# Depthwise taps and layer 3's context in tiles of 32 rows and columns, with new orders and PSUM banks

## The reference

```python
x = x + L0(gn(x))   # attention over rows of C, softmax of 256x256 scores per image
x = x + L1(gn(x))   # batch norm, sign, grouped 3x3 convolution, batch norm, PReLU
x = x + L2(gn(x))   # below
x = x + L3(gn(x))   # linear attention, 8 heads of 16 channels
# L2
h = depthwise_conv3x3(x, dw_w) + dw_b
h = prune(relu(bn(h)), 4.0)         # a channel whose maximum is under the limit becomes 0
h = conv1x1(h, pw_w) + pw_b
h = prune(relu(bn(h)), 0.001)
# L3, per image and head
k = softmax(k, axis=-1)
context = einsum('bhdn,bhen->bhde', k, v)
out = einsum('oc,bcn->bon', w_out, einsum('bhde,bhdn->bhen', context, q)) + b_out
```

## Time and profile before

| | us |
|---|---|
| median of 3 runs | 74.31 (74.23 to 74.63) |
| profiled execution | 74.13 |
| its span | 72.4 |
| TensorE busy | 59.6 (82%) |
| VectorE busy | 47.3 (65%) |
| ScalarE busy | 33.0 (46%) |
| GpSimd busy | 23.9 (33%) |

### The profile page before, as it was taken

How to read it: one execution, slowest core, us unless ns; L and a number is a source line. 1 busy time by engine, 2 the same in 40 slices (tenths; PEclk the granted TensorE clock), 3 DMA queues, 4 the chain that set the end, 5 groups by cost and what they waited for, 6 DMA issues and landing times.

```text
span 72.4 us, 1449 instructions
## 1 busy us (share of the span) xinstructions
PE 59.6 (82%) x472; PEld 46.2 (64%) x472; DVE 47.3 (65%) x182; ACT 33.0 (46%) x98; POOL 23.9 (33%) x67
## 2 busy tenths in 40 slices
PE   3995999799999999399988997899366989968530
PEld 2763787688989878188955663656145869945210
DVE  3959859565688979844579845919869764343430
ACT  5103973958947000570377422402809958642200
POOL 6608899889933335100110043000051340000000
PEclk9999999999999999999999999999999999999995
DMA  0695000000000000000000000000000000002222
GB/s 0 182 407 155 0 0 0 0 0 5 0 0 9 5 0 0 0 0 0 0 0 9 5 0 0 0 9 0 0 0 0 0 5 0 0 9 72 72 72 72
DMA packets 2136, 1.97 MB, mean 27 GB/s; under 512 B 592, under 2 KB 1872, under 8 KB 2128
## 3 DMA queue, kind: packets, MB, share of 16 engines
q1 hardware_dynamic: 2128, 1.87, 7.8%
HBM read 1.35 MB, written 0.52 MB: 26 GB/s over the span
## 4 chain that ended last, share of the span: by engine, by line
PE 53%; DVE 20%; POOL 9%; issue 5%; DMA 5%; ACT 2%; SPq 1%; POOLq 0%; ACTq 0%; DVEq 0%
PE bank L1486 11%; PE bank L1431 6%; PE bank L1418 5%; DMA x<-in_x 5%; POOL gn_rstd L352 4%; DVE t L759 4%; PE bank L1394 4%; PE bank L1560 3%; PE bank L1620 3%; PE bank L1600 3%; PE bank L1405 2%; DVE x L1177 2%; PE bank L1445 2%; PE bank L1579 2%; PE bank L1570 2%
## 5 line engine op out<-in xcount | busy, mean ns | idle before, releaser
L352 POOL TENSOR_TENSOR gn_rstd<-gn_var_eps,minus_half 128x1 f32<-128x1 f32 (+2 forms) x11 | 6.9, 631 | 25.4 <-DVE gn_var_eps L1122 8.5
L1317 PE MATMUL bank<-warm 128*128 128x256 bf16 x36 | 6.7, 349 | 1.2 <-POOL warm L337 1.2
L1317 PEld LDWEIGHTS bank<-warm 128*128 128x128 bf16 x36 | 4.4, 126 | 2.4 <-POOL warm L337 1.2
L1431 PE MATMUL bank<-signs,conv_blocks 128*128 128x256 bf16 x36 | 4.3, 276 | 1.2 <-ACT signs L539 1.2
L539 ACT ACTIVATE signs<-res,bn_shift,bn_scale 128x256 bf16<-128x256 f32 x4 | 2.2, 595 | 6.4 <-DVE bn_shift L932 6.4
L1486 PE MATMUL bank<-t,dw_diag 64*64 64x256 f32 x72 | 4.3, 381 | 0.7 <-DVE t L1046 0.7
L1486 PE MATMUL bank<-x,dw_diag 64*64 64x256 f32 x72 | 4.6, 383 | 0.3 <-DVE x L991 0.3
L1431 PEld LDWEIGHTS bank<-signs,conv_blocks 128*128 128x128 bf16 x36 | 3.4, 97 | 2.2 <-issue 1.6
L1445 PE MATMUL bank<-valid,dw_diag 128*128 128x256 f32 x18 | 4.5, 388 | 0.0
L1394 PE MATMUL bank<-k,q 128*128 128x256 f32 x16 | 4.3, 389 | 0.2 <-DVE k L841 0.2
L1418 PE MATMUL bank<-vt,probT 128*128 128x128 f32 x32 | 4.4, 280 | 0.0
(11 more groups left out here) (196 smaller groups left out, 156.7 us busy)
## 6 DMA issues: line engine op xcount, KB each, us to landing
out<-x SPq DMA_DIRECT2D x4, 128.0 KB, 1.7
late_params<-in_late SPq DMA_DIRECT2D x1, 404.5 KB, 4.5
x<-in_x SPq DMA_DIRECT2D x1, 384.0 KB, 3.4
...
l_params<-in_late SPq DMA_DIRECT2D x3, 4.5 KB, 2.6
```

Of the source, the lines that this page charges most:

```text
L352: return nc.gpsimd.tensor_tensor(out_ap, in_ap, minus_half[:, 0:n], ALU.pow)
L1317: nc.tensor.matmul(bank[:, 0:N], warm[:, 0:C], warm[:, :], start=True, stop=True)
L1431: ins = nc.tensor.matmul(conv_ps[b], conv_w[:, tap, :], signs[:, b, dy:dy + H, dx:dx + W], start=(tap == 0), stop=(tap == TAPS - 1))
```

## The change

- Both pairs' taps run on the raw images in tiles of 32 rows and 32 columns. A row tile r of pair 0 writes the partitions of columns `2i + r % 2`, one of pair 1 those of `2i + 1 - r % 2`; rows 0 and 1 share a bank, and so do rows 2 and 3. The taps of pair 1 stand between those of pair 0. `norm2` and `t2` are gone, and both pairs get `less_mean` and `dw_scale`.
- The channels of pair 1 come out swapped by 32, so `pw2` and the constants of layer 2 get swapped copies by eight more DMAs, and the group sums a swapped matrix `group_swap`.
- `dw_diag` has 32 columns, and one GpSimd operation writes it instead of nine of ScalarE. It needs `ident_tile`, which VectorE makes first of all its statistics. Variances and roots of layer 2, the sums of layer 3 and the reciprocals move to GpSimd.
- The mask's taps run in four diagonal 32x32 tiles.
- In layer 3 all images are handled one by one. Context and its projection run in four tiles of 32 rows; the context has two banks, and so has the output.
- The orders of the tail change on every engine. ScalarE runs `negative_part(2)` ahead of the first square sum, and `relu1(1, 0)` ahead of `square_sum3(0)`.

In the diff a line "..." stands for what is left out.

```diff
     dw_ps = [[banks[i][:, 0:N] for i in pair] for pair in ((3, 4), (0, 1))]
-    pw_ps = [banks[6][:, 0:N], banks[2][:, 0:N]]
+    pw_ps = [banks[i][:, 0:N] for i in (6, 2, 3, 4)]
...
-    k3_ps = [banks[(3, 4)[b % 2]][:, 0:N] for b in range(B)]
+    k3_ps = [banks[(6, 2)[b % 2]][:, 0:N] for b in range(B)]
...
-    pj_ps = banks[2][:, 0:C]
-    y_ps = banks[6][:, 0:N]
+    pj_ps = banks[4][:, 0:C]
+    y_ps = [banks[(6, 2)[b % 2]][:, 0:N] for b in range(B)]
...
-    cx_ps = banks[7][:, 0:C]
+    cx_ps = [banks[(7, 3)[b % 2]][:, 0:TILE] for b in range(B)]
...
+        pw_swap = late[:, LC["pwT"]].rearrange("(r s p) o -> s p r o", r=2, s=2)
+        l2_swap = late[:, first:first + 9].rearrange("(r s p) f -> s p r f", r=2, s=2)
+        for quarter in range(TILES):
+            to = slice(quarter * TILE, (quarter + 1) * TILE)
+            side = 1 - quarter % 2
+            sp.dma_start(pw2[to, 2:4, :], pw_swap[side]).then_inc(halves_in, 16)
+            sp.dma_start(l2p[to, 3:5, :], l2_swap[side]).then_inc(halves_in, 16)
...
-            pool.wait_ge(halves_in, 16 * 5)
+            pool.wait_ge(halves_in, 16 * 13)
...
-                                    ALU.mult, ALU.add)
-            nc.gpsimd.memset(t2[:, :, :, :], 0.0).then_inc(l2_consts, 1)
+                                    ALU.mult, ALU.add).then_inc(l2_consts, 1)
...
+        def group_swaps():
+            there = group_swap[:, :].rearrange("p (h s o) -> p s h o", h=2, s=2)
+            here = group_avg[:, :].rearrange("p (h s o) -> p s h o", h=2, s=2)
+            for side in range(2):
+                ins = nc.gpsimd.tensor_scalar(there[:, side], here[:, 1 - side], 1.0 / N, 0.0,
+                                              ALU.mult, ALU.add)
+            ins.then_inc(group_swap_ready, 1)
+        def dw_diagonals():
+            pool.wait_ge(late_in, 16)
+            pool.wait_ge(ident_tile_ready, 1)
+            nc.gpsimd.tensor_tensor(
+                dw_diag[:, :, :], ident_tile[:, :].unsqueeze(1).to_broadcast([C, TAPS, TILE]),
+                lp[:, LC["dw"]].unsqueeze(2).to_broadcast([C, TAPS, TILE]),
+                ALU.mult).then_inc(dw_diag_ready, 1)
...
+        def gn2_mean_diag(p):
+            pool.wait_ge(group_read[2], p + 1)
+            nc.gpsimd.tensor_tensor(
+                mean_diag[:, p, :, :], ident_tile[:, :].unsqueeze(1).to_broadcast([C, 2, TILE]),
+                gs2[:, p, 4:6].unsqueeze(2).to_broadcast([C, 2, TILE]),
+                ALU.mult).then_inc(mean_diag_ready, 1)
+        def gn2_scale(p):
+            pool.wait_ge(group_read[2], p + 1)
+            step(nc.gpsimd.tensor_tensor(gs2_sq[:, p, :], gs2[:, p, 0:4:2], gs2[:, p, 0:4:2],
+                                         ALU.mult))
+            step(nc.gpsimd.tensor_tensor(ve2[:, p, :], gs2[:, p, 1:4:2], gs2_sq[:, p, :],
+                                         ALU.subtract))
+            step(root(rstd2[:, p, :], ve2[:, p, :]))
+            nc.gpsimd.tensor_tensor(dw_scale[:, p, :], rstd2[:, p, :], l2_scale[:, 3 * p:3 * p + 2],
                                     ALU.mult).then_inc(dw_scale_ready, 1)
-        def gn3_root(b, n, count):
-            pool.wait_ge(var_ready[3], count)
-            root(rstd[:, 3, b:b + n], ve[:, 3, b:b + n]).then_inc(rstd_ready[3], 1)
...
+        def rinv3_out(b):
+            pool.wait_ge(e3_ready, b + 1)
+            nc.gpsimd.tensor_tensor(rinv3[:, b:b + 1], sum3[:, b:b + 1], minus_one[:, :],
+                                    ALU.pow).then_inc(rinv3_ready, 1)
...
+        dw_diagonals()
         l2_constants()
+        group_swaps()
...
-        gn2_root(0)
-        dw_scale_out()
-        gn2_root(1)
-        gn3_root(0, 2, 1)
-        norm_bias_out()
+        gn2_scale(0)
+        gn2_mean_diag(0)
+        gn2_mean_diag(1)
+        gn2_scale(1)
         out_bias_less_floor(0)
+        x3_sum_less_floor(0)
         out_bias_less_floor(1)
-        gn3_root(2, 1, 2)
-        gn3_root(3, 1, 3)
+        x3_sum_less_floor(1)
+        mean_with_floor(0)
+        gn_root(3, 0)
+        norm_bias_out(0)
         out_bias_less_floor(2)
+        x3_sum_less_floor(2)
+        mean_with_floor(1)
         out_bias_less_floor(3)
+        gn_root(3, 1)
+        x3_sum_less_floor(3)
+        norm_bias_out(1)
+        mean_with_floor(2)
+        gn_root(3, 2)
+        mean_with_floor(3)
+        rinv3_out(0)
+        gn_root(3, 3)
+        rinv3_out(1)
+        rinv3_out(2)
+        rinv3_out(3)
...
+        def tile_consts():
+            dve.wait_ge(pool_consts, 1)
+            nc.vector.tensor_reduce(ident_tile[:, :],
+                                    ident[:, :].rearrange("p (g o) -> p o g", g=TILES),
+                                    X_AXIS, ALU.add).then_inc(ident_tile_ready, 1)
...
-        def vars2(p):
-            if p == 0:
-                settle("gs2", 0)
-            else:
-                dve.wait_ge(group_read[2], 2)
-            step(nc.vector.tensor_tensor(gs2_sq[:, p, :], gs2[:, p, 0:4:2], gs2[:, p, 0:4:2],
-                                         ALU.mult), "gs2_sq", p)
-            settle("gs2_sq", p)
-            nc.vector.tensor_tensor(ve2[:, p, :], gs2[:, p, 1:4:2], gs2_sq[:, p, :],
-                                    ALU.subtract).then_inc(var_ready[2], 1)
...
+        h1_out(2)
         x2_first_out(0)
         x2_first_out(1)
-        h1_out(2)
+        x1_h1_out(2)
         h1_out(3)
-        x1_h1_out(2)
         x2_out(2)
         x1_h1_out(3)
         x2_out(3)
-        means2()
-        vars2(0)
...
-        norm2(0)
-        norm2(1)
+        means2(0)
...
         prune1_weights(0, 0)
+        means2(1)
         prune2_max(0)
+        prune2_floor(0)
         prune2_max(1)
-        prune2_floor(0)
         x3_out(0)
+        prune2_floor(1)
+        prune1_max(1, 1)
+        prune1_max(1, 0)
+        prune1_weights(1, 1)
+        prune1_weights(1, 0)
         x3_out(1)
...
-            pe.wait_ge(dw_diag_ready, tap + 1)
+                pe.wait_ge(dw_diag_ready, 1)
             dy, dx = tap // 3, tap % 3
-            ins = nc.tensor.matmul(valid_ps, dw_diag[:, tap, :], valid[:, dy:dy + H, dx:dx + W],
-                                   start=(tap == 0), stop=(tap == TAPS - 1))
+            for r in range(TILES):
+                of = slice(r * TILE, (r + 1) * TILE)
+                ins = nc.tensor.matmul(valid_ps[of], dw_diag[of, tap, :],
+                                       valid[of, dy:dy + H, dx:dx + W],
+                                       start=(tap == 0), stop=(tap == TAPS - 1))
...
+        def tile_of(p, i, r):
+            side = (r % 2, 1 - r % 2)[p]
+            at = (2 * i + side) * TILE
+            return dw_ps[p][r // 2][at:at + TILE]
+        def depthwise(p, tap):
+            if tap == 0:
                 if p == 0:
-                    pe.wait_ge(x2_ready, 2)
+                    pe.wait_ge(dw_diag_ready, 1)
...
+                pe.wait_ge(x2_ready, 2 * p + 2)
+            dy, dx = tap // 3, tap % 3
+            for r in range(TILES):
+                of = slice(r * TILE, (r + 1) * TILE)
+                for i in range(2):
+                    nc.tensor.matmul(tile_of(p, i, r), dw_diag[of, tap, :],
+                                     xs[2][of, 2 * p + i, dy:dy + H, dx:dx + W],
+                                     start=(tap == 0), stop=False)
...
+        def less_mean(p):
+            pe.wait_ge(valid_ready, 1)
+            pe.wait_ge(mean_diag_ready, p + 1)
+            for r in range(TILES):
+                of = slice(r * TILE, (r + 1) * TILE)
+                for i in range(2):
+                    ins = nc.tensor.matmul(tile_of(p, i, r), mean_diag[of, p, i, :],
+                                           valid_sum[of, :], start=False, stop=True)
+                if r % 2 == 1:
+                    ins.then_inc(dw_mm, 1)
...
-            take_bank7(cx_ready, b + 1)
+            if b % 2 == 0:
+                take_bank7(cx_ready, b + 1)
+            elif b == 1:
+                pe.wait_ge(x3_ready, 3)
+            else:
+                pe.wait_ge(cx_ready, b - 1)
             for j in range(2):
-                ins = nc.tensor.matmul(cx_ps, vt3[:, b, j, :], kt3[:, b, j, :],
-                                       start=(j == 0), stop=(j == 1))
+                for g in range(TILES):
+                    of = slice(g * TILE, (g + 1) * TILE)
+                    ins = nc.tensor.matmul(cx_ps[b][of], vt3[:, b, j, of], kt3[:, b, j, of],
+                                           start=(j == 0), stop=(j == 1))
...
-            nc.tensor.matmul(pj_ps, ctxT[:, b, :], lp[:, LC["woutT"]],
-                             start=True, stop=True).then_inc(pj_mm, 1)
+            for g in range(TILES):
+                of = slice(g * TILE, (g + 1) * TILE)
+                ins = nc.tensor.matmul(pj_ps[of], ctxT[of, b, :], lp[of, LC["woutT"]],
+                                       start=True, stop=True)
+            ins.then_inc(pj_mm, 1)
...
         def output(b):
```

(65 more changed lines are left out.)

391 lines of the change are left out of this document (146 added, 245 removed).

## The result

The changed kernel is slower. Its four runs beside the kernel before gave 75.67, 75.88, 77.18 and 78.88 us. The last two ran at a mean granted clock of 0.949 and 0.934 and are left out of the ratio: 1.019, with a 95% interval of 1.011 to 1.026. The forecast was 71.2 us and its range 69.0 to 75.0, so both the sign and the range were wrong. The profiled execution took 75.67 us (before 74.13), its span 73.9.

A forecast was written before the change was run, and what follows sets the result against it. No single engine was held to bound the kernel, but one chain that changes engines. Terms of +1.35, -0.35, -1.9 and -2.1 us summed to -3.0 from 74.13, 71.1 us, forecast as 71.2 for the median, range 69.0 to 75.0.

The forecast's parts named there:

- Part 1: Setup on VectorE and GpSimd: added work ahead of the sw root loses 1.35 us, bounds 0.7 and 2.2.
- Part 2: Known taps of the mask as 36 tiles: no cost, since TensorE waits 1.21 us for the signs afterwards.
- Part 3: Depthwise taps, up to the first relu1: both pairs' tiles run at once, a gain of 0.35 us.
- sixteen in a round would need about 0.1 of its 0.22 us: Depthwise taps: starting sixteen tile records takes about 0.1 us, so they fit in one round of 0.22 us.
- I take full overlap: Depthwise taps: the disjoint tiles of both pairs were assumed to run fully at once, sixteen in a round.
- Rival 1: Depthwise taps: the two pairs don't overlap, adding 2.15 us, so 73.3 us; chance 0.15.
- Rival 2: Mask and pair taps: row tiles writing into one bank take turns, +9.9 and +3.9, about 85 us; chance 0.06.
- Part 4: From relu1 to layer 3: without normalised copies of pair 1 and with new orders, 1.9 us more gained.
- Part 5: Layer 3: two banks each for output and context, new order, less 0.8 for tile-shape changes: gain 2.1 us.
- the 14 that the prediction had named as a sign of being wrong: Layer 3: the prediction would count as wrong if this stage took over 14 us.
- Rival 3: Setup and layer 3: GpSimd's added work and changes of tile shape eat the gains, up to 76.0 us; chance 0.10.
- the 0.16 for slower: Whole kernel: chance given to a slower result, from the second and third rivals.

The follow-up runs named there:

- e16: Changed kernel, setup as it stands, plus 9, 8 and 10 warm TensorE products at the start and ahead of layer 3: 72.74 to 74.00 us, ratio 0.983.
- e5: Changed kernel plus 18 warm products on an unread bank in TensorE's two idle stretches ahead of layer 3: 74.08 to 75.08 us, ratio 1.004.
- e13: Kernel before with only two output banks for layer 3 and VectorE's order for them: 72.03, 73.81, 74.18 and 75.72 us.
- e17: e11 with all of pair 0's taps ahead of pair 1's, tail orders kept: 72.47 us, ratio 0.973.
- e11: Changed kernel with late tile constants, sw root first on GpSimd, warm products (9, 8, 10), and 128x128 context and projection: 72.10 us, ratio 0.963.
- e1: Changed kernel with the reduction for ident_tile moved from ahead of the first statistics to behind the weights' variance: 75.56 us, ratio 1.008.
- e9: e5 with one bank instead of two for layer 3's output: 75.33 us, ratio 1.014.
- e2: Changed kernel with the sw root as GpSimd's first work after x_bias: 72.52, 75.29, 75.51 and 76.57 us.
- e8: e5 with one 128x128 product each in place of four tiles in layer 3's context and projection: 74.27 us, ratio 0.989.

## Why the prediction was wrong

| part | forecast | the kernel after | at full clock |
|---|---|---|---|
| 1 setup, to the signs | +1.35 | +3.08 | +1.6 |
| 3 taps, to `relu1` | -0.35 | +0.87 | +0.56 |
| 4 `relu1` to layer 3 | -1.9 | -1.63 | -1.63 |
| 5 layer 3 | -2.1 | -0.83 | -2.06 |
| sum | -3.0 | +1.5 | -1.5 |

The last column is from `e16`, where the stretches are 6.43, 8.43 and 13.28 us; for the setup, where `e16` itself was 2.76 late by its slow start, it is put together: 1.35 from `x_bias` to the signs, and 0.26 ahead of that (in `e16` the group values are read 0.60 us after the statistics of image 1 start, 0.34 in the kernel before, from 4.67 to 5.01). With the sum, 74.13 becomes 72.6 us, and the two best runs of `e16` are at 72.74 and 72.97. The profiled kernel after missed the sum by 4.5 us. Of these, 1.5 lie in my terms, and 3.0 in what the last column leaves out: 1.5 at the start (TensorE's slow pace, and the statistics of image 1 that waited for their transfer until 5.25 instead of 4.67), 0.3 in the taps, 1.2 in layer 3.

**The clock was missing from the sum.** I priced every product at the durations of full speed, and the earlier trace rows show 1.00, but no step asked what the change does to the idle stretches of TensorE. In the kernel before, layer 3 ran at full clock through a wait of 1.25 us ahead of it. In the changed kernel the tail in front of layer 3 is shorter, with two waits of 1.15 and 1.11 us close together, and the clock falls. The price there is 1.23 us by `e5`. The other part is the slow start, worth up to 1.5 us. It stands in `e13` too, whose setup is unchanged, so luck of the execution has a share in it; but it stands in each of the eight traces of the change without the added products at the start, and in one of the two such traces with the setup of before. So the setup had a second cost that my sum put at nothing: it makes the late clock more likely, and the comparison sets runs of before without it against runs of the changed kernel with it. The Trainium skill, "TensorE: Matmul & The Clock Gate", Part 1, says that one kernel leaves the low clock after a different number of products in different runs. With the same setup the trace of before records the full clock from 5.72 us and `e13` from 13.49, which agrees.

**Part 1** was right in size from `x_bias` on. `sw` root and signs were to come 1.17 us later by GpSimd's work: the stretch from `x_bias` to the start of the root grew from 10.13 to 11.18 us, and to the signs by 1.33. The single terms hold too (`dw_diag` 0.67 for 0.82, the root 0.32 more for 0.3, `group_swap` 0.45). The eight transfers were free as said: each took 0.43 us on SyncE's queue instead of 0.65, and all had landed by 11.02, while GpSimd came to the wait at 15.1.

**Part 2** held: the mask's taps ended before the signs, and TensorE still waited 1.18 us for them.

**Part 3** failed at the sentence "sixteen in a round would need about 0.1 of its 0.22 us", and with it at "I take full overlap". I took the 0.02 us within which four records start as the pace for any number. A tap of one pair is 16 records in two rounds, and seven of them take 3.05 us in `e17` (41.27 to `less_mean` at 44.31), 0.43 each. With the taps of both pairs in flight, the start times of `e11` give 163 records from 42.60 to 45.80 us, and those of the kernel after 98 from 44.90 to 46.90 (the windows' 117 counts 19 more that were already running). That is one in 20 ns and 11 in a round of 0.22, where full overlap needs 16. So a tap of each pair, 32 records, takes 0.60 to 0.65 us instead of 0.43, and the five taps of pair 1 ahead of `less_mean(0)` cost the 0.77 us that separate `relu1` in `e11` and `e17`. Rival 1 priced no overlap at all at 2.15 us, so it came true by a third. Rival 2 didn't: both it and rival 1 in full would show eight starts or fewer in a round. What holds the rounds back isn't shown: in `e11` 16 records start between 43.73 and 43.89, so it is no plain limit on starts. The Trainium skill, "TensorE: Matmul & The Clock Gate", Part 3, gives a packed group one product's duration and about 4 ns for each further tile; the starts of sixteen tiles would by that take 0.06 us (an estimate from the page's figure). The trace disagrees for a long stream.

Without pair 1 beside it the rest of the part would have held: the stretch took 5.40 us in `e17`, 0.47 less than before, where I had forecast 0.35. The taps of pair 1 added 0.77.

A stall in the window 46.95 to 47.35 comes on top, in which no weight load and no product starts and nothing is waited for. The loads pause there for 0.54 us; at the same place of the program they pause for 0.2 to 0.28 in `e1`, `e5`, `e9` and `e16`, and for 0.82 in `e2` and `e8`. In the three long cases a 16 KB transfer of the instruction queue had ended 1.4 us before the pause did, after 1.12 to 1.39 us of its own. In `e16` such a transfer took 1.23 us and the pause stayed short. So instruction fetch is likely and not shown, and no run set it. It is the difference between 6.74 us here and 6.43 in `e16`.

**Part 4** was nearly right as a step (-1.63 for -1.9), but not independent of part 3. Serial taps with the new tail orders reach layer 3 15.78 us after the first tap, and the kernel before took 15.94. The tail orders by themselves are worth 0.16 us; what brings layer 3 forward is that pair 1's taps are done early, 0.97 us. Together 1.13, where the forecast had 2.25 for the two parts.

**Part 5** gave its total at full clock (2.06 for 2.1) by two errors that cancel; that is luck. In the kernel after, layer 3 took 14.51 us, over the 14 that the prediction had named as a sign of being wrong, and the clock is the reason. Everything in it but the tiles gives 2.31 (`e8`, 13.03 against 15.34), not 2.9, and the output banks with their order alone give 2.19 of it (`e13`); the tiles of 32 in context and projection cost 0.25, not 0.8. They gain nothing in either pair of traces, and the changes of shape that the forecast feared are a third of its price.

Rival 3 had the right sign, by the wrong mechanism: setup and changes of shape were both below its bounds. No rival named the clock or an overlap of the two pairs in part, and the 0.16 for slower was too little for a program in which the chain changes engines this often.
